# A float32 mix on TensorE replaced by three float32r products of high and low parts, split a group ahead

## The reference, cut to what matters

```python
# x: (128, 64, 512), adj: (64, 64) of 0/1, symmetric with unit diagonal
W = adj * adj
x = layernorm(x + einsum('bnf,nm->bmf', x, W) + bias)      # the "mix" and layer norm 1
# second layer, h = x, per batch of 64 nodes:
z_l, z_g, v = h @ W_lang.T, h @ W_grav.T, h @ W_V.T
A_l = relu(cosine(z_l, z_l)) * not_eye ; A_g = exp(-d2(z_g) / (2 sigma^2)) * not_eye
K = w * rows_normalised(A_l * adj) + (1 - w) * rows_normalised(A_g * adj)
out = layernorm(h + (K @ v) @ W_O.T)
```

## Time and profile before

| what | value |
|---|---|
| median of 3 runs | 627.45 us (626.82 to 627.95) |
| span of the profiled execution, first to last instruction | 625.0 us |
| what lies around the span, from the median | 2.45 us |
| busy time | PE 614.2, VectorE 444.2, ScalarE 242.7, GpSimd 155.5 us |
| granted TensorE clock, mean | 0.998 |
| one middle iteration | 35.73 us |

### The profile page before, as it was taken

One profiled execution on the slowest core, in us unless ns is written; L12 is line 12 of the kernel. 1 busy time (PEld: TensorE's weight loads), 2 busy tenths in 40 slices (PEclk: granted clock), 3 DMA queues, 4 the chain that ended last, 5 costly groups with the idle time before them and its releaser, 6 DMA issues.

```text
span 625.0 us, 11961 instructions
## 1 busy us (share of the span) xinstructions
PE 614.2 (98%) x4468; PEld 315.0 (50%) x4468; DVE 444.2 (71%) x940; ACT 242.7 (39%) x413; POOL 155.5 (25%) x159
## 2 busy tenths in 40 slices
PE   9999999999999999999999999999999999999994
PEld 6543545454454545454454545445454545545452
DVE  1759486877868586876868687786858788686564
ACT  2345224333443424434432433344342443443333
POOL 1002205032231403123230503223140312323021
PEclk9999999999999999999999999999999999999999
DMA  8722203434123342423223342312334242302103
GB/s 269 244 44 87 51 1 68 136 53 125 52 62 116 64 134 60 141 42 87 90 50 134 67 134 55 120 51 58 119 67 134 59 143 42 92 17 51 69 2 135
DMA packets 89392, 55.05 MB, mean 88 GB/s; under 512 B 70816, under 2 KB 70816, under 8 KB 89376
## 3 DMA queue, kind: packets, MB, share of 16 engines
q1 hardware_dynamic: 19744, 38.05, 17.9%
q10 hardware_dynamic: 69632, 16.79, 13.4%
HBM read 21.27 MB, written 16.78 MB: 61 GB/s over the span
## 4 chain that ended last, share of the span: by engine, by line
PE 96%; DVE 2%; ACT 1%; POOL 0%; issue 0%; POOLq 0%; ACTq 0%; DVEq 0%
PE proj L359 31%; PE proj L375 27%; PE front L339 9%; PE ps_t L389 7%; PE front L429 4%; PE ps_k L429 4%; PE ps_t L400 3%; PE ps_v L409 2%; PE proj L499 2%; PE proj L529 2%; PE ps_v L416 2%; PE ps_t L499 1%; PE ps_k L329 1%; DVE p_lo L736 1%; PE ps_t L529 1%; DVE y L709 0%
## 5 line engine op out<-in xcount | busy, mean ns | idle before, releaser
L557 ACT ACTIVATE p_hi<-proj 128x512 f16<-128x512 f32 x128 | 75.9, 593 | 118.2 <-PE proj L359 117.7
L736 DVE TENSOR_TENSOR p_lo<-proj,p_hi 128x512 f16<-128x512 f32 x128 | 86.0, 688 | 20.9 <-ACT p_hi L557 17.9
L375 PE MATMUL proj<-m_hi,ht_hi 128*128 128x512 f16 x256 | 97.2, 380 | 0.7 <-DVE p_lo L736 0.7
L375 PE MATMUL proj<-m_hi,ht_lo 128*128 128x512 f16 x256 | 97.0, 379 | 0.0
L375 PE MATMUL proj<-m_lo,ht_hi 128*128 128x512 f16 x256 | 97.0, 379 | 0.0
L1026 POOL TENSOR_TENSOR ve<-mv,eps_ln 128x4 f32<-128x4 f32 x31 | 6.6, 212 | 307.7 <-DVE mv L718 211.5
L562 ACT ACTIVATE u<-proj 128x512 f32<-128x512 f32 x64 | 37.9, 592 | 82.7 <-PE proj L375 82.5
L543 ACT ACTIVATE h_hi<-h 128x512 f16<-128x512 f32 x64 | 36.5, 619 | 69.0 <-DVE h L726 69.0
L1065 POOL TENSOR_TENSOR h_lo<-h,h_hi 128x512 f16<-128x512 f32 x30 | 41.5, 1403 | 84.4 <-ACT h_hi L543 84.4
L359 PE MATMUL proj<-ht_hi,l_grav_hi 128*128 128x512 f16 x160 | 60.6, 379 | 0.6 <-DVE p_lo L736 0.6
L359 PE MATMUL proj<-ht_hi,l_lang_hi 128*128 128x512 f16 x160 | 60.8, 380 | 0.0
(11 more groups left out here) (166 smaller groups left out, 1051.8 us busy)
## 6 DMA issues: line engine op xcount, KB each, us to landing
x_in<-in_x SPq DMA_DIRECT2D x16, 1024.0 KB, 7.1
out<-o SPq DMA_DIRECT2D x15, 1024.0 KB, 5.0
w_raw_lang<-in_L_gnn_W_lang SPq DMA_DIRECT2D x4, 256.0 KB, 3.1
o<-in_L_gnn_W_O SPq DMA_DIRECT2D x1, 1024.0 KB, 10.2
w_raw_grav<-in_L_gnn_W_grav SPq DMA_DIRECT2D x4, 256.0 KB, 10.1
u<-in_L_gnn_W_V SPq DMA_DIRECT2D x1, 1024.0 KB, 12.0
ht_hi<-h_hi ACTq DMA_TRANSPOSE x64, 2.4
ht_lo<-h_lo ACTq DMA_TRANSPOSE x64, 2.5
```

The costliest lines, as they stand in the source:

```text
L375: mm = pe.matmul(proj[j % 3][:, :], a[g.parity][:, k, p * P:(p + 1) * P], b[:, k, :], start=(n == 0), stop=(n == len(passes) - 1))
L557: act.activation(p_hi[:, j % 4, :, j // 4, :], by_batch(proj[j % 3]), ACT.Copy).then_inc(phi_ready, 1)
L736: dve.tensor_tensor(p_lo[:, j % 4, :, j // 4, :], by_batch(proj[j % 3]), p_hi[:, j % 4, :, j // 4, :], ALU.subtract).then_inc(plo_ready, 1)
```

## The change

The product wmix by x is written as wmix_hi x_hi + wmix_lo x_hi + wmix_hi x_lo, all of type float32r (a float32 rounded for one of TensorE's formats), accumulated in PSUM. ScalarE writes x_hi (`x_high`), GpSimd subtracts to get x_lo (`x_low`), VectorE makes both parts of wmix once. x_in now has one buffer, and x_hi and x_lo two each. In iteration g the parts of group g+2 are made; x of a group is loaded when the low parts of the group before it are there.

```diff
-        x_in = [sb(f"x_in{i}", [P, PAIRS, D]) for i in range(2)]
+        x_in = sb("x_in", [P, PAIRS, D])
+        x_hi = [sb(f"x_hi{i}", [P, PAIRS, D], F32R) for i in range(2)]
+        x_lo = [sb(f"x_lo{i}", [P, PAIRS, D], F32R) for i in range(2)]
...
             def reload(g):
-                sp.wait_ge(l0_done, g.count(4, 4))
-                load(Group(g.half + 1, g.parity))
+                sp.wait_ge(xlo_ready, g.count(4, 4))
+                load(g.next())
...
-            load(Group(0, 1))
             reload(Group(0, 0))
+            reload(Group(0, 1))
+            reload(Group(1, 0))
+            store(Group(0, 0))
             with sp.Fori(0, G // 2 - 2) as i:
-                reload(Group(i, 1))
-                store(Group(i, 0))
-                reload(Group(i + 1, 0))
+                reload(Group(i + 1, 1))
                 store(Group(i, 1))
+                reload(Group(i + 2, 0))
+                store(Group(i + 1, 0))
             last = G // 2 - 2
-            reload(Group(last, 1))
-            for g in (Group(last, 0), Group(last, 1), Group(last + 1, 0)):
+            for g in (Group(last, 1), Group(last + 1, 0)):
                 store(g)
...
             def mix(g, p, first=False):
-                if p == 0:
-                    pe.wait_ge(x_loaded[g.parity], g.half * 16 + 16)
+                pe.wait_ge(xlo_ready, g.count(4, p + 1))
...
-                pe.matmul(front[p % 2][:, :], wmix[:, :], x_in[g.parity][:, p, :],
-                          start=True, stop=True).then_inc(l0_done, 1)
+                passes = ((wmix_hi, x_hi), (wmix_lo, x_hi), (wmix_hi, x_lo))
+                for n, (w, x_part) in enumerate(passes):
+                    mm = pe.matmul(front[p % 2][:, :], w[:, :], x_part[g.parity][:, p, :],
+                                   start=(n == 0), stop=(n == len(passes) - 1))
+                mm.then_inc(l0_done, 1)
...
+            def x_high(g, first=False):
+                act.wait_ge(x_loaded[g.parity], g.half * 16 + 16)
+                if not first:
+                    act.wait_ge(l0_done, g.prev().prev().count(4, 4))
+                for p in range(PAIRS):
+                    act.activation(x_hi[g.parity][:, p, :], x_in[:, p, :], ACT.Copy).then_inc(xhi_ready, 1)
...
                 if first:
+                    x_high(nxt, first=True)
                     m_high(0)
+                if split_next and not first:
+                    x_high(nxt.next())
                 p_high(g, 0, first)
+                if split_next and first:
+                    x_high(nxt.next())
...
+            x_high(Group(0, 0), first=True)
             for k in range(DC):
                 act.wait_ge(gw_done, k + 1)
...
+            dve.tensor_copy(wmix_hi[:, :], wmix[:, :]).then_inc(wmix_ready, 1)
+            dve.wait_ge(wmix_ready, 1)
+            dve.tensor_tensor(wmix_lo[:, :], wmix[:, :], wmix_hi[:, :], ALU.subtract).then_inc(wmix_ready, 1)
...
+            def x_low(g):
+                for p in range(PAIRS):
+                    pool.wait_ge(xhi_ready, g.count(4, p + 1))
+                    pool.tensor_tensor(x_lo[g.parity][:, p, :], x_in[:, p, :], x_hi[g.parity][:, p, :],
+                                       ALU.subtract).then_inc(xlo_ready, 1)
...
+                if not has_prev:
+                    x_low(g.next())
+                if split_next and has_prev:
+                    x_low(g.next().next())
...
                 if has_next:
                     ln1(g.next())
+                if split_next and not has_prev:
+                    x_low(g.next().next())
+                if has_next:
                     for p in (2, 3):
...
+            x_low(Group(0, 0))
             ln1(Group(0, 0))
```

More of the change, by code:

```diff
@@ L24 @@
 F16 = mybir.dt.float16
+F32R = mybir.dt.float32r
 ALU = mybir.AluOpType
@@ L146, in resnorm_graph_kernel @@
         wmix = sb("wmix", [P, P])
+        wmix_hi = sb("wmix_hi", [P, P], F32R)
+        wmix_lo = sb("wmix_lo", [P, P], F32R)
         not_eye = sb("not_eye", [P, N])
@@ L204, in resnorm_graph_kernel @@
         l0_done = sem("l0_done")
+        xhi_ready = sem("xhi_ready")
+        xlo_ready = sem("xlo_ready")
+        wmix_ready = sem("wmix_ready")
         y_ready = sem("y_ready")
@@ L267, in load @@
             def load(g):
-                sp.dma_start(x_in[g.parity][:, :, :], x_dram[g.half * 2 + g.parity]).then_inc(x_loaded[g.parity], 16)
+                sp.dma_start(x_in[:, :, :], x_dram[g.half * 2 + g.parity]).then_inc(x_loaded[g.parity], 16)
             def store(g):
@@ L314, in run @@
         def run(engine, iteration, back):
[L316 to L320, removed]
+            iteration(Group(0, 0), has_prev=False, has_next=True, split_next=True)
+            with engine.Fori(0, G // 2 - 2) as i:
+                iteration(Group(i, 1), has_prev=True, has_next=True, split_next=True)
+                iteration(Group(i + 1, 0), has_prev=True, has_next=True, split_next=True)
+            iteration(Group(G // 2 - 2, 1), has_prev=True, has_next=True, split_next=True)
+            iteration(Group(G // 2 - 1, 0), has_prev=True, has_next=True, split_next=False)
+            iteration(Group(G // 2 - 1, 1), has_prev=True, has_next=False, split_next=False)
             back(Group(G // 2 - 1, 1))
@@ L444, in back, with iteration @@
                     pe.matmul(last_ku_bank[p][:, :], kt[:, p, :], u[:, p, :], start=(p == 3), stop=True).then_inc(ku_done, 1)
-            def iteration(g, has_prev, has_next):
+            def iteration(g, has_prev, has_next, split_next):
                 first = not has_prev
@@ L507, in _ @@
             pe.wait_ge(dve_const, 3)
+            pe.wait_ge(wmix_ready, 2)
             for p in range(PAIRS):
@@ L957, in _ @@
             dve.tensor_tensor(wmix[GR, GR], adj_sq[GR, :], eye2[GR, :], ALU.add).then_inc(dve_const, 1)
+            dve.wait_ge(dve_const, 3)
+            dve.tensor_copy(wmix_hi[:, :], wmix[:, :]).then_inc(wmix_ready, 1)
+            dve.wait_ge(wmix_ready, 1)
+            dve.tensor_tensor(wmix_lo[:, :], wmix[:, :], wmix_hi[:, :], ALU.subtract).then_inc(wmix_ready, 1)
             dve.tensor_scalar(not_eye[:, :], eye2[:, :], -1.0, 1.0, ALU.mult, ALU.add).then_inc(dve_const, 1)
```

## The result

745.8 us (745.2 to 747.5, 4 runs) against 627.7 us: a ratio of 1.189 (95% interval 1.187 to 1.191). The kernel became 118 us slower where 90 were forecast, and the time lies 8 us above the stated range. The traced execution is the longest of the four, 747.5 us; its span is 745.6 us, 120.6 more than the span before.

What follows compares the result with a forecast made beforehand. TensorE was taken to bound the kernel. Beginning +8.5, iterations 1 and 14 -2 x 0.85, wait for x +65 and clock +18 gave +90 us on 627.45, so 717 us; range 692 to 738.

Steps and rivals of the forecast that it cites:

- The bound and the path: Middle iterations: TensorE alone forms the chain of waits, and lateness of the kernel transpose costs time one for one.
- the wait: Iterations 2 to 13: x_high on ScalarE waits for x, loaded behind a store; transpose 5.4 us late, +65 us.
- The rival in which the load comes in time: All iterations: x is there when ScalarE needs it, iterations 1 to 14 gain 0.85 us each; 624 us, chance 0.06.
- The low parts on GpSimd: Late iterations: four GpSimd subtractions, 5.6 us, delay nothing behind them in its queue, with 1.3 us of cover.
- The clock: Behind TensorE's stall in twelve iterations: clock falls to 1.2 GHz, 1.5 us an iteration, +18 us.
- The rival without a fall: Late iterations: the wait for x as forecast, but the clock stays high; 699 us, chance 0.26.
- the one at half speed to the end of the attention products: Behind the stall in twelve iterations: clock costs 65 us instead of 18; 764 us, chance 0.06.
- The beginning: Prologue and iteration 0: making the first parts delays projection 4 from 53.64 to 61.9; +8.5 us.
- The mix: TensorE: three float32r products take 0.65 us a mix instead of 0.86, 0.85 us less an iteration.
- The rival of 0.43 us a product: TensorE's mixes: a float32r product costs 0.43 us, the stall is 3.7 us, the clock stays; 706 us, chance 0.08.
- The sum: Whole kernel: beginning, iterations 1 and 14, wait for x and clock add to +90 us, 717 us.

Runs made afterwards that it cites:

- e1: Changed kernel with each load issued ahead of the store that stood before it in SyncE's queue; 640.3 us, ratio 1.019.
- e9: Changed kernel, late loads kept, with x_high behind p_high(2) on ScalarE and x_low behind h_lo on GpSimd; 627.8 us, ratio 1.000.
- e4: Changed kernel with the mix cut to its first product, wmix_hi by x_hi, all waits kept; 744.8 us, ratio 1.186.
- e2: Changed kernel, late loads kept, with x_low begun only behind ks_sb, in iteration 0 behind h_lo; 730.1 us, ratio 1.164.
- e3: Changed kernel, late loads kept, with 28 throwaway TensorE products before the kernel transpose in iterations 1 to 13; 726.9 us, ratio 1.157.
- e6: e5 with group 0 mixed by the float32 product and the parts of group 1 made in the prologue; 620.5 us, ratio 0.988.
- e5: Changed kernel with the edits of e1 and e2 together; 627.5 us, ratio 0.9995.
- e7: e6 with the three products in the order hi hi, hi lo, lo hi; 620.2 us, ratio 0.988.

## Why the prediction was wrong, point by point

*The bound and the path: right.* The chain was TensorE's, and the transpose was the point at which lateness counts. The SyncE queue read as text gave the wait, its twelve iterations, its place and its length. The delay of the transpose was forecast as 5.4 us. Measured from the entry of the iteration it stands at 365.24 - 351.0 = 14.2 instead of 8.0, 6.3 us late; without the 1.0 us that ks_sb is held up, 5.3. e1 and e9, which take away the wait in two different ways, and e4, which takes TensorE's work away, show that it is the wait. The rival in which the load comes in time is out: x_high found no data in any of the twelve.

*"The low parts on GpSimd ... Nothing, with 1.3 us of cover": the step that failed.* The forecast asked only when GpSimd would be ready for its next work, and its four subtractions do take 5.4 us for 5.6 forecast and delay no work of its own. It did not ask what runs on VectorE meanwhile. Beside x_low, ks_sb takes 1.65 us for 0.68 and h up to 1.49 for 0.54. That is 12 x 1.0 us, and 3.8 us in iteration 0, with 0.9 for the first h_lo behind them; e2 takes all of this away. The Trainium skill (SBUF — State Buffer, section SBUF: two separate sides) says that a VectorE operation in a two-port mode, or with two SBUF inputs while GpSimd's reads SBUF too, is blocked as a whole by a GpSimd operation that came first. The rule fits the rows: ks_sb (two SBUF inputs) and h (SBUF to SBUF) are stretched, p_lo and y, which read PSUM, keep their 0.69; ks_sb's extra 1.0 us is under one x_lo (1.36), and in iteration 0 four h and four x_lo take turns at 1.4 us each. The runs show which operations collide; whether h runs in a two-port mode, and that the ports are the reason, no run shows.

*The clock: right in kind, too small.* Forecast 1.5 us an iteration with a few falls missing. All twelve fell, and each cost 2.1 (e3) to 2.4 us (the windows): 25 to 29 us for 18. The gap was 6.9 us and not 6.2, from the held-up ks_sb, and the low level lay over 4.8 us of work, not over the 3.7 of the start. The rival without a fall is out, and so is the one at half speed to the end of the attention products: the clock came back 1.2 us after the first of them began.

*The beginning: +8.5 forecast, +14.4 measured.* Up to projection 4 the number is the forecast's (+8.3), but that is luck. Timelines of TensorE and ScalarE, and a window:

```profile
47.91 0.50 PE L351 MATMUL front<-x_hi,wmix_hi 128*128 128x512 f32 x1 [3.54 <-POOL x_lo L1065]
...
71.95 0.61 PE L372 MATMUL proj<-ht_hi,l_grav_hi 128*128 128x512 f16 x1 [5.26 <-DVE p_lo L764]
...
56.83 0.60 ACT L579 ACTIVATE p_hi<-proj 128x512 f16<-128x512 f32 x1 [2.33 <-PE proj L372]
57.32 2.18 ACT L561 ACTIVATE x_hi<-x_in 128x512 fp32r<-128x512 f32 x4
...
49.00:50.00 1.00, 0.84 (x2) 0.75 (x3) 0.61 (x1) 0.00 (x0) 1.00 (x2) 0.58 0.00 0
```

Load 2 was issued at 51.6 and landed 5.0 us later, and ScalarE did not stand before x_high(2) as forecast: it came straight from p_high(0). That copy was late itself, 56.8 for some 53.9, because TensorE's gap of 3.5 us before the mixes was followed by a low clock from 49.2 to 56.0, which the forecast had not priced in the beginning. Two errors met at the same microsecond. Behind projection 4 come the four h with 3.8 us and the first h_lo with 0.9, so projection 6 starts at 71.95 for 58.95, +13.0. Behind that gap the clock is low again, from 69.7 to 76.5, and this makes the last 1.4 us. e6 gets back 7.0 us by restoring the beginning alone, after e5 has taken the held-up operations out.

*The mix: 0.70 us instead of 0.65*, so 0.6 us an iteration where it shows, and it showed in no iteration with x_low beside VectorE: iteration 1 gained 0. The miss of 0.05 us a mix is small beside the other terms. The rival of 0.43 us a product is out.

The sum, forecast in brackets: late iterations 12 x (5.3 [5.4] + 1.0 [0] + 2.4 [1.5]) + 1.9 unassigned (iteration 2, whose load took 8.2 us, has the most of it) = 106.3 [83]; beginning 14.4 [8.5]; iterations 1 and 14 -0.3 [-1.7]. That is 120.4 of the span's 120.6. Of the 30 us above the forecast, some 12 are ks_sb, 11 the clock in the late iterations, and 6 the beginning. None of these alone would have left the range, whose upper end lay 21 us above the forecast; together they did.

## What to carry to other kernels

Write out each queue with its waits for three consecutive iterations before moving work: a load behind a store behind a late result is issued when the result is there, and the first in-order engine that waits for it holds all that is queued behind. Such a wait can be cured at either end (e1, e9), and the second needs no earlier load. Work put on GpSimd has two prices, when GpSimd is free and what VectorE does in those microseconds; here it did no harm beside VectorE's reads of PSUM and its row statistics. A gain on the bounding engine is worth only as much as the slack of every other engine at the next meeting point: in e1 the 0.6 us an iteration were lost there, in e5 they showed.

## What the runs showed of the hardware

- A float32r product of 128x512 takes 0.233 us at 2.4 GHz, against 0.216 for float16 and 0.43 for each of the two instructions of a float32 one; the order of the stationary operands does not matter (e7).
- The granted clock fell 4.8 us after TensorE's last product in the middle iteration shown (4.3 us at the end of the kernel before) and stayed low for 6.8 us, 4.8 of them with TensorE at work. It also fell in iteration 0 at 49.2, 4.8 us after the products that ended at 44.4, although TensorE was at work again from 47.9, after 3.5 us without a product.
- GpSimd's x_lo also held up VectorE's smallest operations: in iteration 1 of the changed kernel degr and degm take 0.74 and 0.73 us for 0.15 and 0.16, while row statistics beside it keep 0.68. In e2, where x_lo comes later, neither takes over 0.17 in any iteration.
